# Edge stage of a graph kernel: gathers and scatters of a group issued in turn

## The chip, the cores and the metric

The kernel runs on one core of one Trainium2 chip. A core has five engines that each follow a program of their own and meet at semaphores: TensorE (PE in the rows; PEld are its weight loads), VectorE (DVE), ScalarE (ACT), GpSimd (POOL) and SyncE (SP). Sixteen DMA engines move data between HBM and SBUF. The metric is the device time of one execution in microseconds, as a median of several runs.

## The reference

```python
# x [12500, 64], src and dst [200000] (dst is sorted), edge_attr [200000, 32]
future_out = mlp(concat(x[dst], edge_attr), W1f, b1f, W2f, b2f)
future_agg = segment_sum(future_out, src)
past_out = mlp(concat(x[src], edge_attr), W1p, b1p, W2p, b2p)
past_agg = segment_sum(past_out, dst) / max(count(dst), 1)
x = layernorm(x + mlp(concat(past_agg, future_agg)) + x)
h = two sage layers over the same edges: segment_sum(x[src], dst) / degree, two products, norm, relu
x = layernorm(x + h)
```

The sums over `dst` run over a sorted list, those over `src` over a random one. The rows `x[src]` have to be gathered one by one, and the sums `future_agg` have to be scattered one by one.

## The kernel before

The program has a set-up, the edge stage, a combination over the nodes, and two sage layers. The change lies in the edge stage alone. It takes the 200000 edges in 391 groups of 512, and a group in four tiles (q = 0 to 3) of 128 edges, one edge to a partition. For each group:

- GpSimd gathers `x[src]` into `gbuf[b]`, one indirect DMA for each tile (line 651), with the indices in `gidx[b]`. The buffer b is the parity of the group.
- TensorE turns the gathered rows into `psX` (line 960, semaphore s_X), and ScalarE copies them to `srcT` (line 855).
- TensorE computes the hidden layers (lines 970, 977, 978) and then, one step later, the sums over `dst` (lines 884, 887) and the sums of equal `src` within a tile (`equal_sums`, line 918, semaphore s_D). ScalarE copies the latter to `sbuf[b]` (line 845, semaphore s_sb).
- VectorE makes the destination rows `sidx[b]` (line 739, semaphore s_sidx), and for the first 240 groups it also makes ranks for the later stages (among others a scan at line 763 and a product at line 770).
- GpSimd scatters `sbuf[b]` with an accumulating indirect DMA for each tile into four tables in HBM, `future[q]` (line 665, semaphores s_sc[0] to s_sc[3]).

All engines run the same loop over groups, written out by `over_groups`; each is a row of instructions in fixed order. In step g GpSimd waits until TensorE has turned group g - 1 (its buffer is free then) and until the indices of group g + 1 stand in `gidx`. It issues the four gathers of group g + 1. Then it waits for three things: the scatters of group g - 2 have landed (two accumulating scatters into one table may not overlap), `sidx` and `sbuf` of group g - 1 are there. It issues the four scatters of group g - 1. TensorE in its step g waits at line 960 for all four gathers of group g, then makes the sums of group g - 1, whose result ScalarE copies to `sbuf`, and after them the products of group g. So the gathers of GpSimd's step g - 1 are needed by TensorE before it can make the sums that GpSimd's step g scatters.

In what follows g0 to g3 are the gathers of a step and s0 to s3 its scatters.

Of the kernel before, what the change touches and what calls it, by code (L numbers as in the profile page):

```python
# [29 lines left out]
TILES = 4  # L30
GROUP = TILES * P
GROUPS = -(-E // GROUP)
# [45 lines left out]
def build(nc, x, src, dst, ea, W1f, b1f, W2f, b2f, W1p, b1p, W2p, b2p, Wc1, bc1, Wc2, bc2,  # L78
# [11 lines left out]
    with ctx:  # L90
        def sb(name, shape, dt=F32):
            return ctx.enter_context(nc.sbuf_tensor(name, shape, dt))
# [3 lines left out]
        def tmp(name, shape, dt=F32):  # L96

            return stage[0].enter_context(nc.sbuf_tensor(name, shape, dt))
# [24 lines left out]
        def sem(name):  # L123
            return ctx.enter_context(nc.semaphore(name))
# [49 lines left out]
        gidx = sb("gidx", [P, 2, TILES], I32)  # L174
# [87 lines left out]
        with nc.Block() as block:  # L262
            @block.sync
            def _(sp):
                for i in range(XPARTS):
                    own = slice(i * XC, (i + 1) * XC)
                    sp.dma_start(x_all[:, own, :], x_p[:, own, :]).then_inc(sA_x[i], 16)
                for to, frm in WEIGHTS:
                    sp.dma_start(to, frm).then_inc(s_weights, 16)
                sp.wait_ge(s_blk16, 1)  # L270
                for c in range(3):
                    g0, g1 = 98 * c, min(98 * c + 98, PEG)
                    sp.dma_start(blkrow[g0:g1, :], blk16[0:g1 - g0, c, :]).then_inc(s_blkst, 16)
                sp.wait_ge(s_blkst, 48)
                for i in range(XPARTS):
                    own = slice(i * XC * CH, (i + 1) * XC * CH)
                    sp.wait_ge(sA_T, (i + 1) * XC)
                    sp.dma_start(xT[:, own], xT_all[:, own]).then_inc(sA_xT[i], 16)
# [219 lines left out]
        gbuf = tmp("gbuf", [P, 2, TILES, D])  # L498
# [40 lines left out]
        s_gat = [sem(f"s_gat{b}") for b in range(2)]  # L539
# [46 lines left out]
        def over_groups(eng, step):  # L586

            def one(g, pair, b, early):
                step(g, pair, b, early, lambda back: 0 <= g - back < PEG)

            one(0, 0, 0, True)
            one(1, 0, 1, True)
            with eng.Fori(1, RANKED) as i:
                step(2 * i, i, 0, False, lambda back: True)
                step(2 * i + 1, i, 1, False, lambda back: True)
            one(PEG, RANKED, 0, False)
            one(PEG + 1, RANKED, 1, False)
            one(PEG + 2, RANKED + 1, 0, False)
            one(PEG + 3, RANKED + 1, 1, False)
            with eng.Fori(RANKED + 2, PAIRS) as i:  # L600
                step(2 * i, i, 0, False, lambda back: False)
                step(2 * i + 1, i, 1, False, lambda back: False)
            one(GROUPS - 1, PAIRS, 0, False)

        def final(g):
            return isinstance(g, int) and g == GROUPS - 1
# [13 lines left out]
        with nc.Fori(0, rounds) as r:  # L620
            with nc.Block() as block:
# [24 lines left out]

                @block.gpsimd
                def _(pool):
                    def gathers(b):
                        for q in range(TILES):  # L650
                            pool.indirect_dma_start(  # L651
                                out=gbuf[:, b, q, :], out_offset=None, in_=x[:, :],
                                in_offset=bass.IndirectOffsetOnAxis(ap=gidx[:, b, q:q + 1], axis=0)).then_inc(s_gat[b], 16)

                    def scatters(g, b):
                        if isinstance(g, int) and g == 0:
                            pool.wait_ge(sA_zeroed, 16 * PARTS * TILES)
                        if not (isinstance(g, int) and g == 0):
                            for q in range(TILES):
                                pool.wait_ge(s_sc[q], r * added + 16 * g)  # L660
                        pool.wait_ge(s_sidx, g + 1)
                        pool.wait_ge(s_sb, g + 1)
                        pool.sem_inc(s_scdone, 1)
                        for q in range(TILES):
                            pool.indirect_dma_start(  # L665
                                out=future[q][:, :],
                                out_offset=bass.IndirectOffsetOnAxis(ap=sidx[:, b, q:q + 1], axis=0),
                                in_=sbuf[:, b, q, :], in_offset=None, compute_op=ALU.add).then_inc(s_sc[q], 16)

                    pool.wait_ge(s_gidx, 1)  # L670
                    gathers(0)
                    pool.memset(featT[W + DE:W + DE + 1, :, :], 1.0).then_inc(s_ones, 1)
                    pool.memset(srcT[D:D + 1, :, :], 1.0).then_inc(s_ones, 1)

                    def step(g, pair, b, early, ranked):
                        if not final(g):
                            if not (isinstance(g, int) and g == 0):
                                pool.wait_ge(s_X, g)
                            pool.wait_ge(s_gidx, g + 2)
                            pool.sem_inc(s_open, 1)  # L680
                            gathers(1 - b)
                        if not (isinstance(g, int) and g == 0):
                            scatters(g - 1, 1 - b)

                    over_groups(pool, step)
                    scatters(GROUPS - 1, 0)
                    for q in range(TILES):
                        pool.wait_ge(s_sc[q], r * added + added)

# [1184 lines left out]
```

## Time and profile before

| | us |
|---|---|
| median of 3 runs | 7693.83 |
| lowest and highest | 7691.86, 7711.77 |
| the profiled execution | 7695.09 |
| its span, first to last instruction | 7693.3 |
| edge stage in that span | about 110 to 5150 |

The profile is of one execution. Busy time counts an engine's work alone, not the issue of instructions or its waits. A timeline row gives start, duration, engine, line, operation, tiles, and in brackets the idle time of that engine ahead of it with what ended it; "issue" means that nothing the profile shows was waited for. For an indirect DMA on GpSimd the duration is the engine's own part, the making of the descriptors; the data move after it.

### The profile page before, as it was taken

What the parts mean: (1) busy time and instruction counts of PE and PEld (TensorE: products, weight loads), DVE (VectorE), ACT (ScalarE), POOL (GpSimd) and SP (SyncE); (2) the same over time, 40 slices, a digit from 0 to 9 for tenths busy, and PEclk for the clock granted to TensorE, in tenths of its full rate; (3) what the DMA queues carried; (4) which work ended last, traced back from release to release, by engine and by line L of the source; (5) the groups of instructions that cost most, each with busy time, mean ns of one, the idle gap of its engine ahead of it and who ended that gap; (6) DMA issues with size and microseconds to landing.
All of it is one profiled execution on the core that took longest, in us unless ns stands there. A gap on an engine that the chain in (4) does not pass through costs nothing. (4 is left out here: it accounts for less than half of the span.)

```text
span 7693.3 us, 142775 instructions
## 1 busy us (share of the span) xinstructions
PE 6764.5 (88%) x40296; PEld 5280.2 (69%) x40296; DVE 4537.4 (59%) x17372; ACT 2229.5 (29%) x4883; POOL 5906.4 (77%) x4715
## 2 busy tenths in 40 slices
PE   5998999989889998898999988987999996999993
PEld 4777877878778877787788877865555554555552
DVE  5777777777777777633333333336666664666663
ACT  2222222222222222222222222226333334333333
POOL 5888888888888888888888888864788784877873
PEclk7777777776777777766666677668999996999995
DMA  4333333333333333322222222223333334323342
GB/s 132 34 35 33 34 35 34 34 34 34 34 34 34 34 34 33 33 28 27 28 27 27 27 28 27 27 38 120 75 73 76 75 71 72 74 74 77 75 71 53
DMA packets 718022, 374.05 MB, mean 49 GB/s; under 512 B 550672, under 2 KB 668197, under 8 KB 717459
## 3 DMA queue, kind: packets, MB, share of 16 engines
q0 software_dynamic: 319648, 158.18, 20.6%
q1 hardware_dynamic: 395649, 210.89, 10.7%
q8 instruction: 121, 1.98, 0.1%
q10 hardware_dynamic: 2482, 2.00, 0.1%
q14 instruction: 122, 1.00, 0.0%
HBM read 289.60 MB, written 81.09 MB: 48 GB/s over the span
## 5 line engine op out<-in xcount | busy, mean ns | idle before, releaser
L665 POOL DMA_INDIRECT future<-sbuf,sidx x1564 | 2497.4, 1597 | 486.9 <-issue 453.8
L651 POOL DMA_INDIRECT gbuf<-in_x_dram,gidx x1564 | 1592.0, 1018 | 481.5 <-issue 471.9
L1571 PE MATMUL bank<-at_dst,rows 128*128 128x512 bf16 x3136 | 1204.9, 384 | 0.5 <-ACT rows L1538 0.5
L1573 PE MATMUL bank<-at_dst,rows 128*128 128x512 bf16 x3136 | 1201.9, 383 | 0.0
L1538 ACT CAST rows<-bank 128x384 bf16<-128x384 f32 x1568 | 751.2, 479 | 1224.8 <-PE bank L1557 1224.1
L1422 POOL DMA_INDIRECT gb<-x,nidx x640 | 794.1, 1241 | 243.2 <-issue 147.6
L1422 POOL DMA_INDIRECT gb<-h,nidx x640 | 781.5, 1221 | 245.7 <-issue 143.9
L1460 DVE TENSOR_SCALAR at_dst<-iota,metaf 128x512 bf16<-128x512 f16 x3136 | 942.2, 352 | 3.1 <-PE bank L1573 1.4
L977 PEld LDWEIGHTS bank<-w1pe,featT 96*128 96x128 f32 x3128 | 727.7, 271 | 308.6 <-issue 308.0
L978 PE MATMUL bank<-w1px,srcT 65*128 65x128 f32 x3128 | 820.7, 356 | 0.0
L977 PE MATMUL bank<-w1pe,featT 96*128 96x128 f32 x3128 | 820.7, 356 | 0.0
L960 PE MATMUL bank<-ident,gbuf 128*64 128x128 f32 x1564 | 299.4, 325 | 456.0 <-DMA gbuf<-in_x_dram,gidx 455.7
L978 PEld LDWEIGHTS bank<-w1px,srcT 65*128 65x128 f32 x3128 | 685.8, 270 | 0.0
L970 PE MATMUL bank<-featT,wwin 97*128 97x512 f32 x782 | 627.7, 897 | 0.0
L918 PE MATMUL bank<-msg,equal 128*128 128x64 f32 x3128 | 614.7, 360 | 0.0
L1557 PEld LDWEIGHTS bank<-wide,at_src 128*128 128x128 bf16 x3136 | 296.7, 99 | 422.4 <-DVE at_src L1453 71.5
L1557 PE MATMUL bank<-wide,at_src 128*128 128x192 bf16 x3136 | 523.6, 249 | 70.6 <-DVE at_src L1453 70.6
L918 PEld LDWEIGHTS bank<-msg,equal 128*128 128x128 f32 x3128 | 549.9, 265 | 36.6
L884 PE MATMUL bank<-comb,hid 128*128 128x64 f32 x3128 | 554.2, 337 | 0.0
L960 PEld LDWEIGHTS bank<-ident,gbuf 128*64 128x64 f32 x1564 | 164.1, 127 | 547.8 <-issue 538.3
L884 PEld LDWEIGHTS bank<-comb,hid 128*128 128x128 f32 x3128 | 521.5, 252 | 2.8
L830 DVE TENSOR_TENSOR hid<-hid,bank 128x512 f32<-128x512 f32 x391 | 266.1, 681 | 435.8 <-ACT hid L865 434.9
(260 smaller groups left out, 11120.4 us busy)
## 6 DMA issues: line engine op xcount, KB each, us to landing
laneb<-lanes SPq DMA_DIRECT2D x448, 224.0 KB
gbuf<-in_x_dram,gidx POOLq DMA_INDIRECT x1564
comb<-in_edge_attr_dram SPq DMA_DIRECT2D x391, 64.0 KB
future<-sbuf,sidx POOLq DMA_INDIRECT x1564, 3.2
blkb<-blkrow SPq DMA_DIRECT2D x240, 98.0 KB
future<-zero POOLq DMA_DIRECT2D x16, 800.0 KB, 17.9
fut<-future SPq DMA_DIRECT2D x100, 125.0 KB
gb<-x,nidx POOLq DMA_INDIRECT x644, 2.7
```

The lines of the kernel that those rows point to most:

```text
L651: pool.indirect_dma_start(out=gbuf[:, b, q, :], out_offset=None, in_=x[:, :], in_offset=bass.IndirectOffsetOnAxis(ap=gidx[:, b, q:q + 1], ...
L665: pool.indirect_dma_start(out=future[q][:, :], out_offset=bass.IndirectOffsetOnAxis(ap=sidx[:, b, q:q + 1], axis=0), in_=sbuf[:, b, q, :], ...
L884: pe.matmul(psS[:, 0:W], hidp[:, b, q * P:(q + 1) * P], comb[:, b, q, 0:W], start=(q == 0), stop=(q == TILES - 1))
L918: last = pe.matmul(psD[:, q * D:(q + 1) * D], equal[:, b, q, :], msg[:, b, q, :], start=True, stop=True)
L977: pe.matmul(psP[:, tile], featT[0:W + DE, b, tile], w1pe[:, :], start=True, stop=False)
L978: last = pe.matmul(psP[:, tile], srcT[:, b, tile], w1px[:, :], start=False, stop=True)
L1422: pool.indirect_dma_start(out=gb1[:, m, q, :], out_offset=None, in_=frm[:, :], in_offset=bass.IndirectOffsetOnAxis(ap=nidx[:, i % 2, m, q: ...
L1460: dve.tensor_scalar(at_dst[:, t % DR, :], iota16[:, :], metaf[:, b:b + 1], None, ALU.is_equal).then_inc(t_at, 1)
L1538: act.copy(rows16[:, j % AR, :, 0:PW], psA[j % AR][:, 0:2 * PW].rearrange("p (h k) -> p h k", h=2)).then_inc(t_cp, 1)
L1557: pe.matmul(psA[j % AR][:, (t % 2) * PW:(t % 2 + 1) * PW], at_src[:, (t // RING) % 2, t % RING, :], pieces[:, b, :], start=True, stop=True ...
L1571: pe.matmul(psHM[i % 2][:, :], rows16[:, j % AR, t % 2, 0:2 * D], at_dst[:, t % DR, :], start=(b == 0), stop=(b == BLOCKS - 1))
L1573: pe.matmul(psL[i % 2][:, :], rows16[:, j % AR, t % 2, 2 * D:4 * D], at_dst[:, t % DR, :], start=(b == 0), stop=(b == BLOCKS - 1)).then_in ...
```

## The change

In place of four gathers and then four scatters, a step issues g0 and g1, then waits for what the scatters need, and then issues g2, s0, g3, s1, s2, s3. The first two groups' gathers and the last scatters keep the old order. A gather gets a function of its own, and `scatters` an argument that says whether gathers stand between.

```diff
--- before.py
+++ after.py
@@ -646,13 +646,16 @@
 
                 @block.gpsimd
                 def _(pool):
+                    def gather(b, q):
+                        pool.indirect_dma_start(
+                            out=gbuf[:, b, q, :], out_offset=None, in_=x[:, :],
+                            in_offset=bass.IndirectOffsetOnAxis(ap=gidx[:, b, q:q + 1], axis=0)).then_inc(s_gat[b], 16)
+
                     def gathers(b):
                         for q in range(TILES):
-                            pool.indirect_dma_start(
-                                out=gbuf[:, b, q, :], out_offset=None, in_=x[:, :],
-                                in_offset=bass.IndirectOffsetOnAxis(ap=gidx[:, b, q:q + 1], axis=0)).then_inc(s_gat[b], 16)
-
-                    def scatters(g, b):
+                            gather(b, q)
+
+                    def scatters(g, b, between):
                         if isinstance(g, int) and g == 0:
                             pool.wait_ge(sA_zeroed, 16 * PARTS * TILES)
                         if not (isinstance(g, int) and g == 0):
@@ -662,6 +665,8 @@
                         pool.wait_ge(s_sb, g + 1)
                         pool.sem_inc(s_scdone, 1)
                         for q in range(TILES):
+                            if between and q < TILES - 2:
+                                gather(b, q + 2)
                             pool.indirect_dma_start(
                                 out=future[q][:, :],
                                 out_offset=bass.IndirectOffsetOnAxis(ap=sidx[:, b, q:q + 1], axis=0),
@@ -678,12 +683,16 @@
                                 pool.wait_ge(s_X, g)
                             pool.wait_ge(s_gidx, g + 2)
                             pool.sem_inc(s_open, 1)
-                            gathers(1 - b)
+                            if isinstance(g, int) and g == 0:
+                                gathers(1)
+                            else:
+                                gather(1 - b, 0)
+                                gather(1 - b, 1)
                         if not (isinstance(g, int) and g == 0):
-                            scatters(g - 1, 1 - b)
+                            scatters(g - 1, 1 - b, not final(g))
 
                     over_groups(pool, step)
-                    scatters(GROUPS - 1, 0)
+                    scatters(GROUPS - 1, 0, False)
                     for q in range(TILES):
                         pool.wait_ge(s_sc[q], r * added + added)
```

GpSimd, the second half of the loop's body in the ranked groups, before (L651 gathers, L665 scatters; L660 raises a counter behind the wait):

```order
L679 REGISTER_ALU
L651 DMA gbuf<-in_x_dram,gidx 128x64 x4
L660 ISA
L665 DMA future<-sbuf,sidx 12800x64 x4
L593 REGISTER_ALU
L593 COMPARE_AND_BRANCH
```

The same place after (L650 gathers, L670 scatters, L663 the counter behind the wait):

```order
L684 REGISTER_ALU
L650 DMA gbuf<-in_x_dram,gidx 128x64 x2
L663 ISA
L650 DMA gbuf<-in_x_dram,gidx 128x64
L670 DMA future<-sbuf,sidx 12800x64
L650 DMA gbuf<-in_x_dram,gidx 128x64
L670 DMA future<-sbuf,sidx 12800x64 x3
L593 REGISTER_ALU
L593 COMPARE_AND_BRANCH
```

The wait with its counter stands behind two gathers in place of four, and the last gather stands behind the first scatter. The other engines' rows are the same but for line numbers, which are 9 higher behind the changed functions.

## Rows read from the trace of the kernel before

**Rows 1.** Busy time by stretch: range, length, each engine's busy us, clock, DMA share, GB/s.

```profile
110.00:3100.00 2990.00, 2714.29 (x16569) 2368.23 (x16568) 2175.19 (x8967) 688.77 (x1383) 2427.41 (x1835) 0.73 0.31 34
3100.00:5150.00 2050.00, 1842.68 (x10374) 1624.71 (x10372) 752.70 (x3259) 479.65 (x963) 1651.11 (x1288) 0.69 0.28 27
```

**Rows 2.** Waits of GpSimd, 300 to 5100 us: total us, times, longest.

```profile
POOL gbuf L651 <- issue: 450.7, 1479, 0.3
POOL future L665 <- issue: 433.1, 1421, 0.3
```

**Rows 3.** Timeline of GpSimd, one group: start us, us, engine, line, operation, tiles, idle before.

```profile
4509.91 1.01 POOL L651 DMA_INDIRECT gbuf<-in_x_dram,gidx  x1 [0.30 <-issue]
4511.23 0.98 POOL L651 DMA_INDIRECT gbuf<-in_x_dram,gidx  x1 [0.30 <-issue]
4512.52 0.94 POOL L651 DMA_INDIRECT gbuf<-in_x_dram,gidx  x1 [0.30 <-issue]
4513.77 0.95 POOL L651 DMA_INDIRECT gbuf<-in_x_dram,gidx  x1 [0.30 <-issue]
4515.02 1.62 POOL L665 DMA_INDIRECT future<-sbuf,sidx  x1 [0.30 <-issue]
4516.95 1.58 POOL L665 DMA_INDIRECT future<-sbuf,sidx  x1 [0.30 <-issue]
...
4520.69 1.55 POOL L665 DMA_INDIRECT future<-sbuf,sidx  x1 [0.30 <-issue]
4522.55 1.02 POOL L651 DMA_INDIRECT gbuf<-in_x_dram,gidx  x1 [0.30 <-issue]
```

**Rows 4.** Busy time by stretch, from line 960 to line 960 of three groups.

```profile
2478.80:2493.80 15.00, 14.53 (x71) 13.04 (x72) 9.02 (x38) 2.73 (x5) 12.26 (x10) 0.55 0.32 33
2493.80:2508.80 15.00, 15.00 (x74) 12.87 (x73) 9.65 (x40) 2.99 (x6) 12.19 (x10) 0.54 0.30 32
2508.80:2517.30 8.50, 8.50 (x74) 7.55 (x73) 7.63 (x37) 2.99 (x6) 6.74 (x6) 1.00 0.22 24
```

**Rows 5.** Instructions of lines 960, 845 and 665: what 960 waits for; counts; landing.

```profile
  DMA gbuf<-in_x_dram,gidx: 455.7, 153
...
L845 ACT COPY sbuf<-bank x391: 372/372/373, 121.7 to 5143.4; 128x256 f32<-128x256 f32 x196
...
DMA to landing us min/median/max: 3.0/3.2/5.0
```

**Rows 6.** Timeline of the first two groups of rows 4, all engines.

```profile
2476.46 1.02 POOL L651 DMA_INDIRECT gbuf<-in_x_dram,gidx  x1 [0.30 <-issue]
...
2479.27 0.60 PE L960 MATMUL bank<-ident,gbuf 128*64 128x128 f32 x4 [2.67 <-DMA gbuf<-in_x_dram,gidx]
...
2484.46 0.37 ACT L845 COPY sbuf<-bank 128x256 f32<-128x256 f32 x1 [3.98 <-PE bank L918]
...
2487.96 1.28 DVE L763 TENSOR_TENSOR_SCAN count<-member,carry 98x512 f32<-98x512 f16 x1
...
2500.16 0.37 ACT L845 COPY sbuf<-bank 128x256 f32<-128x256 f32 x1 [4.33 <-PE bank L918]
...
2503.11 1.62 POOL L665 DMA_INDIRECT future<-sbuf,sidx  x1 [0.30 <-issue]
```

**Rows 7.** Timeline of GpSimd: a gather behind gathers, a scatter behind scatters.

```profile
108.85 0.95 POOL L651 DMA_INDIRECT gbuf<-in_x_dram,gidx  x1 [0.16 <-issue]
...
5133.02 1.55 POOL L665 DMA_INDIRECT future<-sbuf,sidx  x1 [2.71 <-ACT sbuf L845]
```

**Rows 8.** Groups of GpSimd, scatters and gathers from 300 to 3100, gathers and scatters from 3300.

```profile
L665 POOL DMA_INDIRECT future<-sbuf,sidx x860 | 1381.8, 1607 | 262.1 <-issue 248.4 <-DVE sidx L739 13.7
L651 POOL DMA_INDIRECT gbuf<-in_x_dram,gidx x860 | 895.2, 1041 | 262.1 <-issue 259.6 <-ACT sbuf L845 2.4
...
L665 POOL DMA_INDIRECT future<-sbuf,sidx x554 | 876.8, 1583 | 168.9 <-issue 162.1 <-DVE sidx L739 6.7
L651 POOL DMA_INDIRECT gbuf<-in_x_dram,gidx x552 | 538.0, 975 | 168.2 <-issue 166.7 <-DVE sidx L739 1.2 <-ACT sbuf L845 0.3
```

## Prediction

> **What bounds the kernel now.** I read the table by stretches first, then GpSimd's waits, then its row of one group, and last what TensorE waits for. The edge stage runs from 110 to 5150 us [rows 1], 5040 us for 391 groups, 12.89 us for one. The change touches nothing outside it. In both of its stretches TensorE looks busier than GpSimd (2714 us against 2427 us, and 1843 against 1651) [rows 1], but busy time leaves out the 0.30 us ahead of each GpSimd DMA. From 300 to 5100 us GpSimd's idle time stands almost wholly in two rows, 450.7 us in 1479 pieces and 433.1 us in 1421, the longest 0.3 us, both put down to its own issue [rows 2]. It waits for nobody; each DMA costs its duration plus 0.30 us. So GpSimd sets the pace: one clean group, from gather 0 to the next gather 0, takes 4522.55 - 4509.91 = 12.64 us [rows 3].
>
> TensorE is close behind. In stretches of one group each it takes 15.0 us at a granted clock of 0.54 to 0.55 (mostly the lower level, 1.2 GHz) and 8.5 us at 1.00 (2.4 GHz) [rows 4]. At the low clock it is slower than GpSimd and falls behind; at the high clock it catches up and then stands at line 960 for gathered rows, 153 times, 455.7 us in all [rows 5]. What it is behind by is covered by the spare time between the end of ScalarE's copy into sbuf (line 845) and scatter 0 of that group. Between 300 and 5100 us this never runs out today [rows 2].
>
> **The change part by part.** It adds and removes no DMA. In each step GpSimd's row g0 g1 g2 g3, wait, s0 s1 s2 s3 becomes g0 g1, wait, g2 s0 g3 s1 s2 s3.
>
> 1. *The wait comes earlier.* From the end of g3 (4513.77 + 0.95 = 4514.72) to the next g0 are 7.83 us, and from g0 to s0, where the wait stands, 4515.02 - 4509.91 = 5.11 us: 12.94 us for TensorE and ScalarE to turn gathered rows into sbuf [rows 3]. After: g3 ends one scatter later (4516.95 - 4515.02 = 1.93 us), and the wait stands ahead of g2, only 4512.52 - 4509.91 = 2.61 us after g0, 2.50 us earlier. What is left is 12.94 - 1.93 - 2.50 = 8.51 us, 4.43 us less.
>
> What stands behind the wait now is g2 and g3, and TensorE's line 960 waits for these. Two slow groups in a row show the price [rows 6]. g3 ends at 2477.48, line 960 begins at 2479.27, sbuf is full at 2484.83, that is 7.35 us after g3: inside 8.51, no wait. TensorE stays slow, and the next sbuf is full at 2500.53, with s0 at 2503.11: 2.58 us to spare today, 2.58 - 4.43 = -1.85 after. GpSimd waits 1.85 us. The group behind it then finds GpSimd 1.85 us later and has that much more to spare.
>
> I took this difference (s0's start less the end of sbuf) for 383 groups of the 391 whose copies begin between 121.7 and 5143.4 us [rows 5]. In 77 it is under 4.43 us. Were each short group to pay alone, the shortfalls come to 93.4 us; if a wait is credited to the groups behind it until TensorE next stands for a gather, 48 waits with 58.7 us are left. If g3's later end moved TensorE not at all, so that only 2.50 us were lost, 16 groups would be short, by 6.3 us. I take the middle of 93.4 and 58.7, 76 us, less 8 us since part 2 makes every group longer and gives the slow TensorE that much more time: **68 us**, ends 6 and 94. The middle, because a GpSimd wait also delays the next g3, which the credit leaves out.
>
> The other conditions of the same wait hold. The scatters of the step before must have landed: 3.2 us after issue, at the most 5.0 [rows 5]; s3 is issued 4522.55 - 4520.69 = 1.86 us ahead of g0 [rows 3], the wait stands 2.61 us behind g0, so 4.47 us pass. The median has 1.3 us to spare and the one worst landing costs 0.5 us: nothing in the sum.
>
> 2. *More changes of kind.* After scatters, g0 takes 1.01 us and g1 0.98, then 0.94 and 0.95; after gathers, s0 takes 1.62 and s1 1.58, then 1.55 [rows 3]. A gather with only gathers ahead of it takes 0.95 us from the first, a scatter with only scatters ahead of it 1.55, even behind a wait of 2.71 us [rows 7]. So the first DMA after a change of kind costs some 0.07 us more and the second some 0.03, and it isn't the wait that does it. Instead of two changes a group there are four: g3 comes first after a scatter (+0.07), s1 first after a gather (+0.04 on what it pays now), s2 second (+0.03). That is 0.14 us, 54 us over 388 groups, if a run of one DMA costs as much as a run of four; nothing, if it doesn't count. The trace has no run of one. I take 0.08, a little over the middle, as the price per change stands in every group: **31 us**, ends 0 and 54. It lies on GpSimd's path with no cover.
>
> 3. *DMAs stretched by VectorE.* While ranks are made (lines 763 and 770), gathers take 1041 ns in the mean against 975 afterwards, scatters 1607 against 1583: 860 x 0.066 = 57 us and 860 x 0.024 = 21 us [rows 8]. The scan of this stretch starts at 2487.96, 8.69 us after line 960 [rows 6], which is 2.65 us into GpSimd's step, at g2. After the change g0 starts 5.90 us after g3's end (7.83 - 1.93) and line 960 1.79 us after it, so the scan would start 4.58 us into the step, beside s0; when the clock is high it starts sooner and stays beside g2. Part would be saved, and line 770 moves in the same way toward the ends of scatters. I take **0**, ends -57 and +21.
>
> The wait of g0 for TensorE's transposes of two groups earlier and for its indices has a whole step to spare, and the first and the last group keep four and four. Nothing else runs past these DMAs on GpSimd's queue.
>
> Sum: 68 + 31 + 0 = 99 us. The profiled execution took 7695.09 us, so 7794; the median of the runs stands 1.3 us lower, hence **7793 us** (+1.3%).
>
> **The rivals.** *No change that can be measured* (within 0.3%, 23 us, which is about what a measurement of this kernel can tell from none): TensorE's place is set by its own work in 391 - 153 = 238 groups that never stood for a gather [rows 5], so only the 2.50 us are lost (6 us) and a run of one costs nothing: some 10 us, 7704. Against it: the slow runs begin from a gather that TensorE waited for [rows 6], and that gather is later.
>
> *Faster*: the scans fall beside scatters, where they cost nothing, and part of the 78 us of part 3 comes back. It decides if over 23 us are saved beyond the waits and the changes of kind; with 6 and 0 for these and 50 saved, 7650. For it stands the scan's 4.58 us, against it the 58.7 us of waits that the same later TensorE brings.
>
> *Much slower, TensorE starved*: g3's rows land later because they queue behind s0's. With 1 us more lost, 5.4 us, 146 groups are short, by 107 us with credit and 186 alone; with 31 that is 138 to 217 us, some 7870. It decides when s0 lands later than g3 would. Against it: s0 is issued some 1.9 us before g3 and lands 3.2 us after issue [rows 5], 1.3 us into g3's own 2479.27 - 2476.46 = 2.81 us [rows 6].
>
> *The clock stays low*: TensorE waited 2.67 us at line 960, and the stretch that starts there was granted 0.55, the next 0.54 without any wait, then 1.00 [rows 4, 6]. If every longer wait brought such a fall and it lasted, a group would take 15.0 us in place of 12.89: 391 x 2.1 = 825 us, 8520. Against it: at the low clock TensorE doesn't wait at all, and the rows show the clock rising out of that. The Trainium skill (TensorE: Matmul & The Clock Gate, "HAM oscillation — how this bites in real kernels") tells of a kernel whose TensorE waits for a DMA in every tile, loses its clock there and starts each tile slow; by that rule alone the time would be this rival's. The fall to 0.55 behind a wait agrees with it; the return to 1.00 within two groups speaks against its lasting here.
>
> **How the numbers follow.** Forecast 0.70, no change 0.13, faster 0.05, starved 0.10, clock 0.02. The forecast's own range is 7714 (59 us of waits, no price for a change of kind, 40 us of scans saved) to 7862 (94 + 54 + 20). For 8 in 10 I reach down to 7700, which takes in over half of no change, and up to 7870, the middle of starved; left out are faster 0.05, 0.05 of no change, 0.05 of starved and the clock 0.02. Chances: faster by over 0.3% 0.05, within 0.13, slower 0.70 + 0.10 + 0.02 = 0.82.
>
> **What would show it.** Part 1: GpSimd's gathers get waits over 0.3 us put down to ScalarE's sbuf, all at g2, some 50 with 60 to 95 us. Part 2: in a clean group g3 takes 1.0 us and s1 1.62, and the group 12.7 us instead of 12.64. Part 3: the mean of gathers in the first half against the second. Starved: line 960 (969 after) starts over 2 us after g3's end wherever it waits for it. Clock: under 0.69 in the stage. I am wrong if no wait at g2 shows, or if the group is over 0.5 us longer.

## The result and the profile after

| | before | after |
|---|---|---|
| median, us | 7700.44 | 7819.56 |
| lowest and highest, 4 runs each | 7691.86, 7711.77 | 7807.51, 7832.14 |
| profiled execution | 7695.09 | 7832.14 |
| its span | 7693.3 | 7830.3 |

The ratio is 1.0147, 95% interval 1.0132 to 1.0162: slower by 119 us, where 99 us were forecast. The profiled executions lie toward opposite ends of their runs, so the traces show 137 us and not 119.

The page of after answers first. The rows are its span and GpSimd's scatters (line 670) and gathers (line 650): busy us and mean ns, then the idle time ahead of them.

```profile
span 7830.3 us, 142543 instructions
...
L670 POOL DMA_INDIRECT future<-sbuf,sidx x1564 | 2497.6, 1597 | 483.1 <-issue 462.4
L650 POOL DMA_INDIRECT gbuf<-in_x_dram,gidx x1564 | 1596.9, 1021 | 617.2 <-issue 513.1
```

The same two rows in the page of the kernel before are:

```profile
L665 POOL DMA_INDIRECT future<-sbuf,sidx x1564 | 2497.4, 1597 | 486.9 <-issue 453.8
L651 POOL DMA_INDIRECT gbuf<-in_x_dram,gidx x1564 | 1592.0, 1018 | 481.5 <-issue 471.9
```

GpSimd's idle time went from 486.9 + 481.5 = 968.4 to 483.1 + 617.2 = 1100.3 us, 131.9 more, all of it ahead of gathers. Its busy time in these DMAs went from 4089.4 to 4094.5 us, 5.1 more. Together 137.0 us, the difference of the spans. GpSimd sets the pace of the stage, as the prediction had it, and nearly all that was lost are waits.

What the waits are for stands in the rows on the users of sbuf (line 854 after, 845 before) and on line 969 (960 before):

```profile
  POOL gbuf L650: 137.8, 66
  POOL future L670: 2.6, 1
...
  DMA gbuf<-in_x_dram,gidx: 577.0, 168
```

The first row puts 66 pieces of idle time down to ScalarE's copy, some of them the usual 0.3 us and no wait. Added up from the timeline as the idle time above 0.30 us ahead of each g2 (waits of over 0.05 us, here and below), GpSimd waited 125 times for the copy, 123 us in all; before, its idle time came only in pieces of 0.3 us [rows 2]. TensorE stands 121 us longer for gathered rows, 577.0 against 455.7 us [rows 5]: what GpSimd waits comes back to it as idle time.

The timeline of after shows a wait and, behind it, a clean group. Columns are those of [rows 3], with ScalarE's copy among them.

```profile
4504.12 1.02 POOL L650 DMA_INDIRECT gbuf<-in_x_dram,gidx  x1 [0.30 <-issue]
4505.45 0.99 POOL L650 DMA_INDIRECT gbuf<-in_x_dram,gidx  x1 [0.30 <-issue]
4506.97 0.37 ACT L854 COPY sbuf<-bank 128x256 f32<-128x256 f32 x1 [4.02 <-PE bank L927]
4508.26 0.94 POOL L650 DMA_INDIRECT gbuf<-in_x_dram,gidx  x1 [1.82 <-ACT sbuf L854]
4509.50 1.62 POOL L670 DMA_INDIRECT future<-sbuf,sidx  x1 [0.31 <-issue]
...
4518.32 1.01 POOL L650 DMA_INDIRECT gbuf<-in_x_dram,gidx  x1 [0.30 <-issue]
...
4522.17 1.62 POOL L670 DMA_INDIRECT future<-sbuf,sidx  x1 [0.30 <-issue]
4524.10 0.98 POOL L650 DMA_INDIRECT gbuf<-in_x_dram,gidx  x1 [0.30 <-issue]
4525.39 1.58 POOL L670 DMA_INDIRECT future<-sbuf,sidx  x1 [0.31 <-issue]
4527.27 1.57 POOL L670 DMA_INDIRECT future<-sbuf,sidx  x1 [0.30 <-issue]
4529.15 1.56 POOL L670 DMA_INDIRECT future<-sbuf,sidx  x1 [0.30 <-issue]
4531.02 1.02 POOL L650 DMA_INDIRECT gbuf<-in_x_dram,gidx  x1 [0.30 <-issue]
```

Two things are to be seen. The copy ends at 4506.97 + 0.37 = 4507.34, and g2 starts at 4508.26: 0.92 us lie between the release and the DMA, not 0.30. In all 125 waits it is 0.92 to 1.04 us. And the clean group takes 4531.02 - 4518.32 = 12.70 us against 12.64 [rows 3]; g3 takes 0.98 us where it took 0.95, s2 1.57 where it took 1.55, and s1 1.58 as before.

By stretches, the granted clock was 0.73 and 0.69 before [rows 1], and after:

```profile
110.00:3100.00 2990.00, 2641.39 (x16245) 2317.51 (x16243) 2160.20 (x8794) 675.78 (x1357) 2377.11 (x1801) 0.74 0.30 34
3100.00:5150.00 2050.00, 1831.13 (x10062) 1613.00 (x10062) 746.48 (x3251) 463.72 (x931) 1603.91 (x1245) 0.67 0.27 27
```

The first half has a little more clock, the second a little less. Nothing like a clock that stays low.

Gathers and scatters by halves, from 300 to 3100 us and from 3400 to 5150 us, to be read against [rows 8]:

```profile
L670 POOL DMA_INDIRECT future<-sbuf,sidx x845 | 1357.5, 1606 | 258.2 <-issue 251.2 <-DVE sidx L748 7.0
L650 POOL DMA_INDIRECT gbuf<-in_x_dram,gidx x844 | 875.8, 1038 | 311.4 <-issue 263.5 <-ACT sbuf L854 47.9
...
L670 POOL DMA_INDIRECT future<-sbuf,sidx x532 | 842.4, 1583 | 163.1 <-issue 152.1 <-DVE sidx L748 11.0
L650 POOL DMA_INDIRECT gbuf<-in_x_dram,gidx x531 | 524.0, 987 | 222.7 <-issue 185.8 <-ACT sbuf L854 34.2 <-DVE sidx L748 2.7
```

While ranks are made, a gather takes 51 ns more than afterwards (66 before the change) and a scatter 23 ns more (24 before).

### The profile page after: what moved, and what is told of

Read it like the earlier page. It is cut to its first block and busy times, and to the rows that moved or that the text cites. A ratio compares the mean times of both kernels' runs of the same rounds, so it can differ in the third digit from the quotient of the medians.

```text
span 7830.3 us, 142543 instructions
## 1 busy us (share of the span) xinstructions
PE 6779.3 (87%) x40064; PEld 5317.6 (68%) x40296; DVE 4556.4 (58%) x17372; ACT 2229.4 (28%) x4883; POOL 5911.1 (75%) x4715
## 5 line engine op out<-in xcount | busy, mean ns | idle before, releaser
L670 POOL DMA_INDIRECT future<-sbuf,sidx x1564 | 2497.6, 1597 | 483.1 <-issue 462.4
L650 POOL DMA_INDIRECT gbuf<-in_x_dram,gidx x1564 | 1596.9, 1021 | 617.2 <-issue 513.1
L1582 PE MATMUL bank<-at_dst,rows 128*128 128x512 bf16 x3136 | 1201.5, 383 | 14.5 <-issue 1.5
L1580 PE MATMUL bank<-at_dst,rows 128*128 128x512 bf16 x2904 | 1114.2, 384 | 0.0
L969 PE MATMUL bank<-ident,gbuf 128*64 128x128 f32 x1564 | 299.9, 326 | 577.0 <-DMA gbuf<-in_x_dram,gidx 577.0
L731 DVE TENSOR_TENSOR acc<-acc,bank 128x64 f32 x391 | 86.4, 221 | 793.1 <-PE bank L896 793.1
```

Of the source, the lines that this page charges most:

```text
L650: pool.indirect_dma_start(out=gbuf[:, b, q, :], out_offset=None, in_=x[:, :], in_offset=bass.IndirectOffsetOnAxis(ap=gidx[:, b, q:q + 1], ...
L670: pool.indirect_dma_start(out=future[q][:, :], out_offset=bass.IndirectOffsetOnAxis(ap=sidx[:, b, q:q + 1], axis=0), in_=sbuf[:, b, q, :], ...
L1580: pe.matmul(psHM[i % 2][:, :], rows16[:, j % AR, t % 2, 0:2 * D], at_dst[:, t % DR, :], start=(b == 0), stop=(b == BLOCKS - 1))
L1582: pe.matmul(psL[i % 2][:, :], rows16[:, j % AR, t % 2, 2 * D:4 * D], at_dst[:, t % DR, :], start=(b == 0), stop=(b == BLOCKS - 1)).then_in ...
```

## The experiments

The sizes of the waits were the open question: 68 us forecast, with 94 as the upper end, 123 in the trace for sbuf alone. Theory H (hand-over): the spare time can be used only down to the 0.92 us between the end of a copy and the DMA that waits for it, so the groups that are short are those under 4.43 + 0.93 = 5.36 us, not 4.43. Counted anew over the spare times of the kernel before, that gives 104 us (a wait credited to the groups behind it) to 181 us (each group for itself). Theory F is the forecast's count, down to zero: 59 to 94 us. A rival to both is that TensorE is simply fed later.

In the table, idle and busy are the two rows of the page added up, as the difference to the kernel before (968.4 and 4089.4 us), span that to 7693.3 us. Time ratios are each against runs of the kernel before on the same chip.

| run | idle | busy | span | median, us | before, us | ratio, 95% interval |
|---|---|---|---|---|---|---|
| changed kernel | +131.9 | +5.1 | +137.0 | 7819.56 | 7700.44 | 1.0147 (1.0132 to 1.0162) |
| e1 wait early | +56.0 | -1.8 | +50.2 | 7759.73 | 7707.95 | 1.0071 (1.0054 to 1.0088) |
| e2 g3 late | +52.0 | -5.0 | +43.2 | 7747.61 | 7707.95 | 1.0049 (1.0032 to 1.0067) |
| e3 kinds | +4.1 | +49.9 | +50.2 | 7741.15 | 7707.95 | 1.0040 (1.0026 to 1.0054) |
| e4 g3 later still | +510.7 | +84.1 | +594.1 | 8289.31 | 7697.02 | 1.0770 (1.0749 to 1.0792) |
| e5 changed, sums later | +15.0 | +22.2 | +27.6 | 7731.86 | 7707.95 | 1.0039 (1.0026 to 1.0053) |
| e6 before, sums later | +0.3 | -9.7 | -23.6 | 7683.54 | 7697.02 | 0.9990 (0.9980 to 1.0000) |
| e7 scan later | +2.2 | +25.1 | +25.1 | 7721.41 | 7697.02 | 1.0038 (1.0025 to 1.0052) |
| e8 e1, wait split | +43.6 | +9.3 | +61.0 | 7723.32 | 7700.97 | 1.0034 (1.0022 to 1.0047) |
| e9 e1, sums later | +30.4 | -11.7 | +14.0 | 7711.17 | 7700.97 | 1.0022 (1.0009 to 1.0035) |

Where idle and busy don't add up to the span (by up to 14 us), the rest lies outside these DMAs, and nothing is concluded from it. The profiled execution of e8 was its slowest of ten.

**e1, the wait alone.** The order is g0 g1, wait, g2 g3 s0 s1 s2 s3.

```diff
-                            if between and q < TILES - 2:
-                                gather(b, q + 2)
+                            if between and q == 0:
+                                gather(b, 2)
+                                gather(b, 3)
```

> Only the wait moves: g0 g1, wait, g2 g3 s0 s1 s2 s3. The spare time between ScalarE's copy into sbuf and the DMA behind the wait shrinks by 2.50 us, g3 ends where it did, and there are two changes of kind a group. Theory H (the hand-over counts): in the trace of the changed kernel the DMA behind the wait starts 0.9 to 1.0 us after the end of the copy, so a group is short when its spare of before is under 2.50 + 0.93 = 3.43 us: 24 to 29 us of waits in some 26 to 30 groups, 7725 us against 7700. Theory F (as forecast, the spare can be used down to 0): 16 groups, 6 us, 7706 us.

Measured: 52 us slower, twice what H says and far above F. GpSimd's users of sbuf in the trace:

```profile
  POOL gbuf L650: 43.7, 35
```

This row is for idle time put down to sbuf, pieces of 0.3 us included. Adding up, ahead of each g2, the idle time above the 0.30 us and looking at when the copy had ended, there are 72 waits with 54 us. In 31 of them, 25 us, g2 starts 0.92 to 1.04 us after the copy: these are H's 26 to 30 groups with 24 to 29 us, and not F's 16 with 6. The other 41, 29.6 us, are something else. One of them:

```profile
4581.45 1.02 POOL L650 DMA_INDIRECT gbuf<-in_x_dram,gidx  x1 [0.30 <-issue]
4581.53 0.37 ACT L855 COPY sbuf<-bank 128x256 f32<-128x256 f32 x1 [1.96 <-PE bank L928]
4582.77 0.98 POOL L650 DMA_INDIRECT gbuf<-in_x_dram,gidx  x1 [0.30 <-issue]
4584.69 0.94 POOL L650 DMA_INDIRECT gbuf<-in_x_dram,gidx  x1 [0.94 <-issue]
```

The copy ended at 4581.90, 2.79 us ahead of g2, and yet there is 0.94 us of idle time, put down to issue. All of these waits but one come at every ninth group, and most of them end 1.86 us after the last landing of s3 of the step before. e8 and e9 take them up.

**e2, g3 behind s0.** The order is g0 g1 g2, wait, s0 g3 s1 s2 s3.

```diff
-                                gather(1 - b, 1)
+                                gather(1 - b, 1)
+                                gather(1 - b, 2)
...
-                            if between and q < TILES - 2:
-                                gather(b, q + 2)
+                            if between and q == 1:
+                                gather(b, 3)
```

> g0 g1 g2, wait, s0 g3 s1 s2 s3: the wait comes one gather earlier (1.25 us), and g3 stands behind s0 as in the changed kernel (1.93 us): 3.18 us less to spare, four changes of kind a group. Theory H: short below 3.18 + 0.93 = 4.11 us, 45 to 70 us of waits, with 29 us for changes of kind (0.076 us a group in the trace of the changed kernel) 7774 to 7799 us. Theory F: short below 3.18 us, 18 to 22 us, with 29 us 7747 to 7751 us.

Measured: 40 us slower, below both (47 to 51 us by F, 74 to 99 by H). The waits (here ahead of s0), 49 us in 44 groups, are within H's 45 to 70 and over twice F's 18 to 22. The time is lower than their sum with 29 us because the busy time, which should have risen by these 29 us, fell by 5.0: some 30 us of stretching by VectorE went away (see e7). So the waits speak for H, and the total alone would have spoken for F by accident.

**e3, changes of kind alone.** g0 of the next step stands between s2 and s3, and the distance from g3 to the wait is that of the kernel before.

```diff
...
-                            if between and q < TILES - 2:
-                                gather(b, q + 2)
+                            if between and q == TILES - 1:
+                                pool.wait_ge(s_X, g + 2)
+                                pool.wait_ge(s_gidx, g + 4)
+                                pool.sem_inc(s_open, 1)
+                                gather(1 - b, 0)
...
-                            if isinstance(g, int) and g == 0:
-                                gathers(1)
-                            else:
-                                gather(1 - b, 0)
-                                gather(1 - b, 1)
+                            for q in range(0 if isinstance(g, int) and g < 2 else 1, TILES):
+                                gather(1 - b, q)
...
```

> The four changes of kind without the lost spare time: g0 of the next step is issued between s2 and s3, then g1 g2 g3, wait, s0 s1 s2. g3 and the wait stand as far apart as in the kernel before (g0 no longer between them, s3 as before). One gather more in all, whose rows nobody reads. If changes of kind cost what they seem to in the changed kernel: 0.076 us a group, 29 us, 7729 us, and a clean group of 12.69 to 12.70 us. If the 0.076 us belongs to something else (the wait's place): 7700 us and 12.62 us. No wait of GpSimd over 0.4 us by either.

Measured: 33 us slower, with 4.1 us more idle time. A clean group, from the first of the three gathers to the same of the next group:

```profile
4509.80 1.02 POOL L650 DMA_INDIRECT gbuf<-in_x_dram,gidx  x1 [0.30 <-issue]
4511.12 0.98 POOL L650 DMA_INDIRECT gbuf<-in_x_dram,gidx  x1 [0.31 <-issue]
4512.40 0.95 POOL L650 DMA_INDIRECT gbuf<-in_x_dram,gidx  x1 [0.30 <-issue]
4513.65 1.62 POOL L673 DMA_INDIRECT future<-sbuf,sidx  x1 [0.30 <-issue]
4515.58 1.57 POOL L673 DMA_INDIRECT future<-sbuf,sidx  x1 [0.30 <-issue]
4517.45 1.55 POOL L673 DMA_INDIRECT future<-sbuf,sidx  x1 [0.30 <-issue]
4519.31 1.01 POOL L650 DMA_INDIRECT gbuf<-in_x_dram,gidx  x1 [0.31 <-issue]
4520.63 1.57 POOL L673 DMA_INDIRECT future<-sbuf,sidx  x1 [0.30 <-issue]
4522.51 1.02 POOL L650 DMA_INDIRECT gbuf<-in_x_dram,gidx  x1 [0.31 <-issue]
```

It takes 4522.51 - 4509.80 = 12.71 us against 12.64, 0.07 us or 27 us over 388 groups. The gather behind scatters takes 1.01, the scatter behind it 1.57, and the next gather again 1.02: a run of one sets the gathers' price back, while the scatter behind the single gather takes 1.57 and not 1.62. With the spare time kept, GpSimd doesn't wait; the rest of the 49.9 us of busy time is one gather more (1.3 us) and stretching.

**e4, g3 one scatter later still.** The order is g0 g1, wait, g2 s0 s1 g3 s2 s3.

```diff
-                            if between and q < TILES - 2:
-                                gather(b, q + 2)
+                            if between and q == 0:
+                                gather(b, 2)
+                            if between and q == 2:
+                                gather(b, 3)
```

> The changed kernel with g3 one scatter later still: g0 g1, wait, g2 s0 s1 g3 s2 s3. 6.31 us less to spare than before the change (4.43 + 1.88), four changes of kind (29 us). Counted over the spare times of the kernel before, with a wait credited to the groups behind it until TensorE next stands for a gather. Theory H (0.93 us of hand-over count): short below 7.24 us, 347 us, 8076 us. Theory F: short below 6.31 us, 218 us, 7947 us.

Measured: 592 us slower, over both. The timeline has a wait of the usual kind (10.90 to 11.82 is 0.92 us again), VectorE's scan, and s1 behind it:

```profile
2010.53 0.37 ACT L856 COPY sbuf<-bank 128x256 f32<-128x256 f32 x1 [4.34 <-PE bank L929]
2011.82 0.94 POOL L650 DMA_INDIRECT gbuf<-in_x_dram,gidx  x1 [2.34 <-ACT sbuf L856]
2013.07 1.62 POOL L672 DMA_INDIRECT future<-sbuf,sidx  x1 [0.31 <-issue]
2014.38 1.28 DVE L774 TENSOR_TENSOR_SCAN count<-member,carry 98x512 f32<-98x512 f16 x1
2015.00 2.05 POOL L672 DMA_INDIRECT future<-sbuf,sidx  x1 [0.30 <-issue]
2017.35 1.22 POOL L650 DMA_INDIRECT gbuf<-in_x_dram,gidx  x1 [0.30 <-issue]
```

And these rows are what GpSimd waits for sbuf, and TensorE for gathers:

```profile
  POOL gbuf L650: 594.3, 286
...
  DMA gbuf<-in_x_dram,gidx: 731.9, 342
```

GpSimd waits in 276 groups and TensorE stands for a gather in 342 of 391, so each side waits for the other. The counts of H and F both rest on groups in which TensorE is behind through its own work; here it no longer is. The round trip sets the pace: from the end of the copy at 2010.90 to the end of g3 at 2017.35 + 1.22 = 2018.57 are 7.67 us, then the rows have to arrive and TensorE has to make the next sums. So the counting method holds only while few groups wait; it says nothing of this run.

**e5 and e6, the sums of equal sources first.** TensorE makes sbuf's sums ahead of the sums over dst, in the changed kernel (e5) and in the kernel before (e6).

```diff
-                            sums(g - 1, 1 - b, ranked)
-                            equal_sums(g - 1, 1 - b)
+                            equal_sums(g - 1, 1 - b)
+                            sums(g - 1, 1 - b, ranked)
```

> The changed kernel with one exchange on TensorE: the sums of equal sources (line 927, which feed sbuf) ahead of the sums over dst (lines 889 to 896), so that sbuf is full 1.6 us earlier at the high clock and some 2.9 us at the low one. GpSimd's order is that of the change. If GpSimd's waits for sbuf are the larger part of the loss: they fall from 138 us (66 waits) to under 20, 7735 to 7750 us, what is left being the changes of kind. If the loss comes from TensorE being fed later by g3, whatever GpSimd waits for: 7800 to 7830 us as before.

> The kernel before with the exchange of e5 on TensorE alone. GpSimd waits for nobody there, so an earlier sbuf gives nothing: 7700 us within 0.3%, no wait of GpSimd over 0.4 us. If it is faster or slower by over 25 us, the exchange does something of its own (VectorE's work falls beside other DMAs), and the result of e5 has to be read against it.

Measured: e5 7731.86 us, e6 7683.54 us. In e5 the users of sbuf are:

```profile
  POOL gbuf L650: 18.0, 17
```

GpSimd's order is that of the change, g3 is as late as there, and the idle time in this row has gone from 137.8 us in 66 pieces to 18.0 in 17 (waits of 123 us to 15). Time falls with them, from 1.0147 to 1.0039 of the kernel before. So the waits for sbuf are the larger part of the loss; TensorE is fed as late here and shows no large loss of its own. e6 has nothing to gain from an earlier sbuf and doesn't (its interval touches 1.0000). Against e6 the change costs 0.49%, some 38 us: 15 us of idle time that are left and the changes of kind.

**e7, the scan later.** VectorE's scan in the kernel before, moved behind the second maximum.

```diff
-                        if ranked(0):
-                            count_members(g, pair, b)
                         dve.wait_ge(s_pslope, g + 1)
                         dve.tensor_tensor(hidp[:, b, :], hidp[:, b, :], psP[:, :], ALU.max).then_inc(s_hp, 1)
                         if ranked(0):
+                            count_members(g, pair, b)
                             own_rank(g, b)
```

> The kernel before with VectorE's scan (and the two instructions that feed it) behind the second maximum instead of ahead of it, so that it starts some 2 to 3 us later, beside scatters. If a scan costs GpSimd time beside a gather and none beside the first half of a scatter, as the stretched durations show: gathers of the first 240 groups lose most of their 65 us of stretching, 7640 to 7665 us. Rival: the scatters are stretched instead, or TensorE waits for the ranks (line 880) and comes later: 7690 to 7720 us.

Measured: 24 us slower, at the upper end of the rival: the scatters are stretched instead. Scatters and gathers from 300 to 3100 us, to be read against [rows 8]:

```profile
L665 POOL DMA_INDIRECT future<-sbuf,sidx x854 | 1407.0, 1648 | 260.3 <-issue 226.8 <-DVE sidx L739 33.5
L651 POOL DMA_INDIRECT gbuf<-in_x_dram,gidx x852 | 874.9, 1027 | 259.6 <-issue 255.0 <-ACT sbuf L844 3.7 <-DVE sidx L739 0.9
```

Gathers gain 14 ns in the mean (1041 to 1027), scatters lose 41 (1607 to 1648). The stretching isn't gone, it moved to scatters and grew. The rows of e4 show how: a scan that starts 0.62 us ahead of s1 gives it 2.05 us instead of 1.58. That a scan beside scatters costs nothing was read from the one place where it happened to start early within a scatter. The Trainium skill (SBUF — State Buffer, "SBUF: two separate sides") says that a VectorE instruction with two SBUF inputs and a GpSimd one that reads SBUF shut each other out for a whole instruction, whichever comes first. The kinds of DMA make no difference there, and e7 agrees. The whole instruction isn't borne out: in the rows of e4 the scan begins 0.31 us before the end of s0, and yet s0 takes its 1.62 us and the scan its 1.28; s1 begins 0.66 us before the end of the scan and loses 0.47.

**e8 and e9, the waits at every ninth group.** e8 is e1 with the wait for the landing of s3 moved ahead of the next s3; e9 is e1 with the exchange of e5.

```diff
-                            for q in range(TILES):
+                            for q in range(TILES - 1):
                                 pool.wait_ge(s_sc[q], r * added + 16 * g)
                         pool.wait_ge(s_sidx, g + 1)
                         pool.wait_ge(s_sb, g + 1)
-                        pool.sem_inc(s_scdone, 1)
+                        pool.sem_inc(s_open, 1)
...
+                            if q == TILES - 1:
+                                if not (isinstance(g, int) and g == 0):
+                                    pool.wait_ge(s_sc[q], r * added + 16 * g)
+                                pool.sem_inc(s_scdone, 1)
```

> e1 with one change: the wait ahead of g2 is no longer for the last scatter of the step before (into table 3); that one is waited for just ahead of s3, five DMAs later. In e1, 41 waits of some 0.6 us (29.5 us) came when sbuf had long been full, each some 1.86 us after that scatter's last landing, at every ninth group. Theory L (the wait is for this landing): they are gone, 30 us fewer waits, 7725 us, and 20 to 25 us of waits for sbuf stay. Theory I (something in GpSimd's own row of instructions that comes every ninth group): they stay, 7750 to 7760 us.

> e1 with the exchange of e5 on TensorE: sbuf is full 1.6 to 2.9 us earlier. The waits for sbuf, 22 us in 31 groups of e1, go to under 3 us by theory H and F alike, since 2.50 us of lost spare time is then covered. The waits at every ninth group, which aren't for sbuf, stay with 25 to 35 us: 7710 to 7735 us against 7684 for e6, which has the exchange without the earlier wait. If they go too, they were waits for sbuf after all: 7685 to 7700 us.

Measured: e8 7723.32 us, 0.34% over the kernel before where e1 is 0.71% over it (some 28 us less), and e9 7711.17 us. Counted as in e1, e8 has 32 waits with 29 us that end 0.92 us after the copy and only 9 others, 11 us; e9 has 2 of the first sort with 0.2 us and 42 of the second with 24 us. So the first sort goes when sbuf is earlier, and the waits for s3's landing go when that wait is elsewhere.

What is left in e8 shows that the ninth group isn't tied to the landing. All 9 others are in ninth groups and end 1.81 us after the copy. One of them:

```profile
3202.27 0.98 POOL L650 DMA_INDIRECT gbuf<-in_x_dram,gidx  x1 [0.30 <-issue]
3203.26 0.37 ACT L859 COPY sbuf<-bank 128x256 f32<-128x256 f32 x1 [4.33 <-PE bank L932]
3205.44 0.94 POOL L650 DMA_INDIRECT gbuf<-in_x_dram,gidx  x1 [2.19 <-issue]
```

The copy ends at 3203.63 and g2 starts 1.81 us later, where it starts 0.92 us later in the other groups. The same holds in e2 (7 waits, 1.83 to 1.84 us) and for 8 of e1's 41 (1.81 to 1.93 us). So in e1, e2, e8 and e9 GpSimd resumes some 0.9 us later at every ninth group, whatever it waited for. That also says why e1's wait for s3's landing costs nothing in the other eight: s3 lands 3.15 us (median) after its start, and with 0.92 us more GpSimd is ready 4.07 us after it, ahead of g2's place at 4.47; with 1.86 us it is 5.01. What comes every ninth group isn't settled. It is hardly the loading of instructions: the DMA queues for instructions moved 7 packets between 300 and 5100 us in e1. In the changed kernel and in e4 no ninth group is late (15 and 27 waits there end 0.92 to 1.04 us after the copy like the rest), and why stays open. With the 0.9 us of its ninth groups taken off, e8 has 32 us of waits for 2.50 us of lost spare time, where H has 24 to 29 us and F 6.

## Why the prediction was right, point by point

The direction, the range (7700 to 7870) and the mechanism hold: 7819.56 measured, 7793 forecast. That the middle came within 27 us is in part luck: part 1 was put 55 us too low, and some 20 us of stretching that part 3 put at nothing were saved against it.

*GpSimd sets the pace.* Right: idle and busy time of its DMAs add up to the span's difference, 131.9 + 5.1 = 137.0 us.

*Part 1, the wait comes earlier: 68 us, ends 6 and 94.* The mechanism is right (e5: take the lateness of sbuf away and the waits go) but the term is mis-sized: 123 us of waits for sbuf in the profiled execution, above its upper end, and 125 waits, where some 50 were expected. The step that failed is the count of groups with under 4.43 us to spare, down to zero. What GpSimd needs is 0.92 us more, the time from the end of the copy to the start of the DMA. The rows to see it stood in the trace of before: [rows 7] has a scatter that waited 2.71 us for sbuf, and the copy it waited for is the first row here:

```profile
5131.76 0.37 ACT L845 COPY sbuf<-bank 128x256 f32<-128x256 f32 x1 [4.02 <-PE bank L918]
5133.02 1.55 POOL L665 DMA_INDIRECT future<-sbuf,sidx  x1 [2.71 <-ACT sbuf L845]
```

5133.02 - 5132.13 = 0.89 us. Counted with 0.93 this term would have been 104 to 181 us; the trace lies in it, nearer to the credited end. e1, e2 and e8, without the 0.9 us of their ninth groups, come near that count for their own losses of spare time (28, 43 and 32 us against 24 to 29, 45 to 70 and 24 to 29) and far above the count down to zero (6, 18 to 22 and 6).

*The landing of the scatters.* "Nothing in the sum" is right for the changed kernel, but with less room than the working gave: 0.92 us from the release to the DMA count here too, and leave 0.4 of the 1.3 us. That no ninth group is late there is luck: with the same 4.47 us from s3's issue to the wait, e1 waited in 32 ninth groups for the landing, 18 us.

*Part 2, changes of kind: 31 us, ends 0 and 54.* The size is right: 0.06 us in a clean group of after and 0.07 in e3, 23 to 27 us. It is spent elsewhere than said: g3 takes 0.98 us, under the 1.0 of the sign, and s1 1.58 as before, not 1.62; s2 and s3 pay 0.01 to 0.02 each. So a run of one sets the price back, but only in part.

*Part 3, stretched DMAs: 0, ends -57 and +21.* Inside its ends: busy time rose by 5.1 us where part 2 alone adds 23 to 27, so some 20 us were saved; the rows by halves give 844 x 0.051 + 845 x 0.023 = 62 us of stretching against 78, 16 saved. The reason given for a saving, that a scan beside a scatter costs nothing, fell with e7.

*The rivals.* No change and faster are out by the time. TensorE starved: its sign was line 969 over 2 us after the end of g3; where TensorE stood for the gather, it began 1.6 us after it (median), 1.93 at the most. That g3's rows queue behind s0's is thus not seen. In e4, one scatter further, TensorE does starve, but by g3's late issue. The low clock: 0.74 and 0.67 after against 0.73 and 0.69 speaks against it. The Trainium skill's rule on it (TensorE: Matmul & The Clock Gate, "HAM oscillation — how this bites in real kernels") tells of a kernel in which each wait for a DMA costs TensorE its clock; here TensorE waits 121 us longer, and the mean clock of the stage hardly moves.

No version here beats the kernel before: e6 is at 0.9990 of it with an interval up to 1.0000.

## What to carry to other kernels

Where an engine issues back to back and sets the pace, the order of its row is free only as long as no wait in it comes due; count the spare time of each wait over all iterations before moving it, and count it down to the hand-over (the time from the release to the start of the instruction that waited) that the trace shows at a wait that did come due, not to zero. Moving a wait ahead of work that the other side needs (here g2 and g3) shortens the loop between the two engines from both ends, and once most iterations wait, the round trip sets the pace and such a count no longer holds. Keep DMAs of one kind together on GpSimd if nothing is gained by mixing them: here two more changes of kind cost 0.06 to 0.07 us a group.

## What the runs showed of the hardware

- From the end of a ScalarE copy to the start of a GpSimd DMA that waits for it are 0.89 to 1.04 us, in the kernel before, in the changed one and in e4; a DMA that doesn't wait follows the one before it after 0.30 us.
- An indirect DMA of 128 rows costs GpSimd 0.95 us as a gather and 1.55 us as an accumulating scatter behind its own kind, and 1.01 and 1.62 us behind a run of the other kind. Behind a single one of the other kind it is 0.98 (changed kernel) to 1.02 us (e3), and 1.57 (e3) to 1.58 (changed kernel).
- VectorE's scan stretches a scatter that starts 0.62 us behind it from 1.58 to 2.05 us (e4); moved off the gathers it cost more beside scatters: 14 ns less for a gather in the mean, 41 ns more for a scatter (e7).
- In e1, e2, e8 and e9 a GpSimd DMA that had to wait starts 1.81 to 1.93 us after the end of a copy, or mostly 1.86 us after a scatter's landing, at every ninth group; in the changed kernel and e4 the ninth groups have 0.92 to 1.04 us like the others. The cause is open.
